# Row-maximum scores from 64 contracted rows, two query chunks side by side in the array, one maximum instruction for both

## The chip, the cores and the metric

The kernel runs on one core of one Trainium2 chip. The metric is the device time of one execution in microseconds (us), the median of several runs. A core has five engines with queues of their own: TensorE (PE, with its weight loads as PEld), VectorE (DVE), ScalarE (ACT), GpSimd (POOL) and SyncE (SP). They meet only at semaphores. Matrix products go to PSUM, which has eight banks of 512 fp32 values per partition; everything else lies in SBUF.

## The reference, cut to what matters

Two transformer blocks follow each other on 2 sequences of 512 tokens of width 128. The change touches the attention of the second one: 16 heads of 64 values, with a normalisation of every query and key.

```
qkv = (h @ Wqkv.T).reshape(b, n, 3, H, HD)
q = _ln(qkv[:, :, 0].transpose(0, 2, 1, 3), qn_g, qn_b)
k = _ln(qkv[:, :, 1].transpose(0, 2, 1, 3), kn_g, kn_b)
v = qkv[:, :, 2].transpose(0, 2, 1, 3)
scores = jnp.einsum('bhnd,bhmd->bhnm', q, k) / jnp.sqrt(jnp.float32(HD))
attn = jax.nn.softmax(scores, axis=-1)
o = jnp.einsum('bhnm,bhmd->bhnd', attn, v)
x = x + o.transpose(0, 2, 1, 3).reshape(b, n, H * HD) @ Wout.T
```

Before it stands a block with one attention head and a wide layer, behind it a gated choice of tokens for 8 experts. Neither is touched.

## The kernel before

The middle of the program, from about 85 to 350 us, handles 32 **units**: one head of one sequence each (`UNITS = 32`, sequences change every second unit). All engines run the same loop of units, each with an order of its own that is written out by hand in a function `time(u, r, head)`. Units 4 to 27 run in a counted loop whose body holds 12 units; the others are written out. In the turn of unit `u` the engines work on up to four neighbours at once: unit `u` gets its row maxima, unit `u-1` its probabilities and products with the values, unit `u-2` is added to the output, and the pieces `u+2` and `u+3` of later queries and keys are made. A **piece** holds two heads' queries and keys for half of the tokens, so a pair of units needs a pair of pieces.

What happens to a piece: `project` (L1426) multiplies tokens and weights in six matmuls; ACT takes squares (L637) and a copy (L643); DVE sums the squares (L977); POOL makes the scale (L484, L488) and applies it (L507); PE turns the result (`turn_piece`, L1231 called from L1436) into bank 1; ACT applies gain and bias (`piece_affine`, L660), which frees the bank and is told by the semaphore `kq_affine`. Keys lie in partitions 0 to 63 and queries in 64 to 127. DVE rounds both to the fast matmul type (`piece_high`, L991, into `k_s`); POOL takes what rounding left off (`piece_low`, L498); ACT copies the rounded queries to partitions 0 to 63 of `q_s` (`q_high`, L666) and the rounded keys to partitions 64 to 127 of `k_s` (`k_high_beside`, L683). So `q_s` holds high and low parts of the queries above each other, and `k_s` the high part of the keys twice.

What happens to a unit: `scores` (L1445) makes, for each of four chunks of 128 queries, one matmul of 128 contracted rows by 512 keys into bank 0; DVE takes the negated row maximum (`row_max`, L1003). With one bank, chunk `c+1` waits for the maximum of chunk `c` (`max_done`). When all four maxima are there, PE transposes them (`shifts`, L1453) into bank 1, and DVE writes them into the rows of `q_shift` (`shift_row`, L1010). `scores_T` (L1459 and L1464) makes the scores again, transposed and in full precision and already lowered by the maximum, into banks 2 and 3 in turn; ACT takes the exponential (L689); `mix` (L1474) multiplies by the values and sums in banks 4 and 5, 8 matmul instructions per call; DVE divides and adds (`unit_out`, L1020 and L1025).

What orders it all is each engine's own queue: PE starts its work strictly in the order of `time` (L1486), ACT in that of L691, DVE in that of L1032, POOL in that of L511.

Of the kernel before, what the change touches and what calls it, by code (L numbers as in the profile page):

```python
# [37 lines left out]
def film_attention_then_expert_choice(  # L38
# [35 lines left out]
    with ctx:  # L74
# [118 lines left out]

        moe = Area(loop2_start)
# [65 lines left out]
        o_rec_done = sem("o_rec_done")  # L260
# [287 lines left out]
        def _(act):  # L548
# [119 lines left out]

            def q_high_beside(p, p_in):

                wait(act, q_hi_moved, p + 1)
                wait(act, st_done, pair_free(p, p_in))
                act.activation(piece_at(q_shift, p_in, 0, HD), piece_at(q_s, p_in, 0, HD).bitcast(F32), ACT.Copy)\
                   .then_inc(q_beside, 1)

            def k_high_beside(p, p_in):

                if isinstance(p, int) and p in (0, 1, 3):
                    act.wait_ge(q_low_done, min(p + 1, 3))
                else:  # L680
                    wait(act, lows_done, 2 * p + 1)
                wait(act, q_hi_moved, p + 1)
                act.activation(piece_at(k_s, p_in, HD, P), piece_at(k_s, p_in, 0, HD).bitcast(F32), ACT.Copy)\  # L683
                   .then_inc(split_done, 1)
# [6 lines left out]
            def time(u, r, head):  # L691
# [18 lines left out]
                if turning:  # L710
                    q_high(u + 2, r + 2)
                if back:
                    keys_exp(u - 1, 3)
# [13 lines left out]
            q_high(0, 0)  # L727
            piece_affine(1)
            k_high_beside(0, 0)
            q_high(1, 1)  # L730
            k_high_beside(1, 1)
# [14 lines left out]
            q_high(2, 2)  # L746
            piece_square(4)
            piece_affine(3)
            keys_exp(0, 2)
            q_high(3, 3)  # L750
            k_high_beside(2, 2)
# [72 lines left out]
        def _(dve):  # L824
# [174 lines left out]
            def row_max(u, c):  # L999
                wait(dve, s_done, 4 * u + c + 1)  # L1000
                if c == 0:
                    wait(dve, shift_done, u)
                dve.tensor_reduce(negmax[:, c:c + 1], bank[0][:, :], AX, ALU.max, negate=True).then_inc(max_done, 1)  # L1003
# [28 lines left out]
            def time(u, r, head):  # L1032
                live, turning, leaving = due(u, 0, UNITS - 1), due(u, 0, UNITS - 3), due(u, 2, UNITS + 1)
                if live:
                    row_max(u, 0)
                if leaving:
                    unit_out(u - 2, r - 2, 0)
                if live:
                    row_max(u, 1)
                if leaving:  # L1040
                    unit_out(u - 2, r - 2, 1)
                if live:
                    row_max(u, 2)
                if due(u, 0, UNITS - 4):
                    piece_ss(u + 3)
                if turning:
                    piece_high(u + 2, r + 2)
                if live:
                    row_max(u, 3)
                    shift_row(u, r)  # L1050
# [16 lines left out]
            row_max(0, 1)  # L1067
            dve.wait_ge(h_act, 6)
            split_h(N + N // 2, TOK)
            row_max(0, 2)  # L1070
            piece_ss(2)
            row_max(0, 3)
            piece_ss(3)
            shift_row(0, 0)
            piece_norm(2, 2)
            row_max(1, 0)
            piece_norm(3, 3)
            piece_high(2, 2)
            row_max(1, 1)
            row_max(1, 2)  # L1080
# [3 lines left out]
            row_max(1, 3)  # L1084
# [142 lines left out]
        def _(pe):  # L1227
# [203 lines left out]
            def turn_piece(p, p_in):  # L1431

                wait(pe, normed, p + 1)
                wait(pe, kq_affine, p)
                wait(pe, shift_copied, p - 2)
                turn4(turn_bank(p), [qk_n[:, p_in % 2, 2 * c + h, :, :].rearrange("p t d -> p (t d)")  # L1436
                                     for h in range(2) for c in range(2)]).then_inc(kqT_done, 1)

            def scores(u, r, c):

                if c == 0:
                    wait(pe, split_done, u + 2 - r % 2)
# [43 lines left out]
            def time(u, r, head):  # L1486
                live, back = due(u, 0, UNITS - 1), due(u, 1, UNITS)
                if live:
                    scores(u, r, 0)
# [3 lines left out]
                if live:  # L1493
                    scores(u, r, 1)
# [5 lines left out]
                if live:  # L1500
                    scores(u, r, 2)
# [7 lines left out]
                if back:  # L1509
                    mix(u - 1, r - 1, 0)  # L1510
                    mix(u - 1, r - 1, 1)
                if live:
                    scores(u, r, 3)
                if back:
                    scores_T(u - 1, r - 1, 3)
                    mix(u - 1, r - 1, 2)
# [16 lines left out]
            keep_busy(1, bank[3])  # L1533
            scores(0, 0, 1)
            keep_busy(2, bank[3])
            pe.wait_ge(h_split, 3)
            project(2, 2, 0)
            scores(0, 0, 2)
            pe.wait_ge(h_split, 4)
            project(3, 3, 0)  # L1540
            scores(0, 0, 3)
            keep_busy(2, bank[3])
            shifts(0, 0)
            scores(1, 1, 0)
# [5 lines left out]
            scores(1, 1, 1)  # L1550
            project(4, 4, 2)
            turn_piece(3, 3)
            scores(1, 1, 2)
            scores_T(0, 0, 2)
            mix(0, 0, 0)
            mix(0, 0, 1)
            scores(1, 1, 3)
            scores_T(0, 0, 3)
# [209 lines left out]
```

## Time and profile before

| | |
|---|---|
| median of 3 runs | 431.98 us (431.81 to 432.7) |
| the profiled execution | 431.72 us |
| its span, first to last instruction | 430.0 us |
| granted TensorE clock, mean | 0.996 |
| PE busy | 405.9 us (94%), 2730 instructions |
| ACT busy | 284.7 us (66%) |
| DVE busy | 273.2 us (64%) |
| POOL busy | 191.9 us (45%) |

The shares are of the span. PE's busy time counts a matmul from its start to a modelled end, and matmuls overlap, so it hides small gaps; the distance between the starts of neighbours tells more. A row of the timeline merges instructions of one kind that follow without a gap: its start, the time to the end of the last, and the count.

### The profile page before, as it was taken

To read this page: it belongs to the slowest core of one execution; us is meant where nothing else is said; L and a number is where in the kernel's file an instruction comes from. 1 tells how busy PE (TensorE), PEld (TensorE's weight loads), DVE (VectorE), ACT (ScalarE), POOL (GpSimd) and SP (SyncE) were. 2 spreads that over 40 slices of the span, in tenths; PEclk is the share of its full clock that TensorE was granted. 3 is DMA by queue.
4 is the path that set the end of the run, shared out by engine and by line. 5 is a ranking of instruction groups with operands and counts; after the bars stand their busy time and mean duration, and the time that the engine had idled before them with its cause. 6 is when DMAs were issued, how large, how long until landed. Compare 5 with 4: busy or idle time off the path is not lost.

```text
span 430.0 us, 8319 instructions
## 1 busy us (share of the span) xinstructions
PE 405.9 (94%) x2730; PEld 341.3 (79%) x2730; DVE 273.2 (64%) x649; ACT 284.7 (66%) x532; POOL 191.9 (45%) x197
## 2 busy tenths in 40 slices
PE   6989997999999999999999999999999897889896
PEld 5678666778888888889888888888888686666694
DVE  3566456767666766666666667666765627986633
ACT  3356566677777777777777777777776337759341
POOL 7400416485566756765765667567656000100000
PEclk9899999999999999999999999999999999999999
DMA  6760000190000000000000000000000000000001
GB/s 128 205 135 1 2 2 0 54 366 23 0 3 2 0 2 1 3 0 2 3 2 0 0 0 1 0 0 0 1 0 2 0 2 1 2 2 2 1 2 49
DMA packets 7792, 10.67 MB, mean 25 GB/s; under 512 B 403, under 2 KB 4302, under 8 KB 7758
## 3 DMA queue, kind: packets, MB, share of 16 engines
q1 hardware_dynamic: 6718, 9.73, 7.9%
q10 hardware_dynamic: 1040, 0.52, 0.4%
q8 instruction: 17, 0.28, 0.3%
q14 instruction: 17, 0.14, 0.1%
HBM read 8.68 MB, written 0.52 MB: 21 GB/s over the span
## 4 chain that ended last, share of the span: by engine, by line
PE 82%; DVE 9%; POOL 4%; issue 2%; ACT 2%; DVEq 0%; POOLq 0%; ACTq 0%
PE pair L1474 26%; PE pair L1426 10%; PE pair L1445 8%; PE bank L1464 6%; PE bank L1459 6%; PE pair L1231 4%; PE pair L1706 2%; PE pair L1315 1%; PE pair L1600 1%; PE pair L1391 1%; PE bank L1231 1%; POOL rstd L453 1%; PE pair L1655 1%; PE pair L1340 1%; PE bank L1695 1%
## 5 line engine op out<-in xcount | busy, mean ns | idle before, releaser
L1474 PE MATMUL pair<-v_s,probs_T 128*128 128x129 f32 x1024 | 128.4, 275 | 0.6 <-ACT probs_T L689 0.6
L1474 PEld LDWEIGHTS pair<-v_s,probs_T 128*128 128x128 f32 x1024 | 124.5, 191 | 4.7 <-ACT probs_T L689 0.9
L1003 DVE TENSOR_REDUCE negmax<-pair 128x1 f32<-128x512 f32 x128 | 88.2, 689 | 50.1 <-PE pair L1445 49.9
L689 ACT ACTIVATE probs_T<-bank 128x512 f32<-128x512 f32 x128 | 73.1, 596 | 49.7 <-PE bank L1464 39.5
L498 POOL TENSOR_TENSOR q_s<-kq,k_s 64x512 fp32r<-64x512 f32 x29 | 37.2, 1283 | 78.0 <-DVE k_s L991 78.0
L1445 PE MATMUL pair<-k_s,q_s 128*128 128x512 f32 x128 | 59.4, 464 | 2.5 <-DVE negmax L1003 2.5
L488 POOL TENSOR_TENSOR qk_rstd<-qk_ms,minus_half 128x8 f32<-128x8 f32 x32 | 53.1, 1661 | 2.6 <-POOL qk_ms L484 0.2
L1459 PE MATMUL bank<-q_s,k_s 128*128 128x512 f32 x128 | 50.9, 397 | 0.0
L1464 PE MATMUL bank<-q_shift,k_low 128*128 128x512 f32 x128 | 50.6, 396 | 0.2 <-DVE q_shift L1010 0.2
L1025 DVE SCALAR_TENSOR_TENSOR x_att<-pair,o_rec,x_att 128x128 f32<-128x128 f32 x128 | 38.6, 345 | 1.1
L498 POOL TENSOR_TENSOR k_low<-kq,k_s 64x512 fp32r<-64x512 f32 x29 | 36.7, 1266 | 2.2
L1010 DVE TENSOR_TENSOR q_shift<-pair,own_chunk 4x512 fp32r<-4x512 f32 x32 | 21.8, 682 | 23.9 <-PE pair L1453 23.9
L1445 PEld LDWEIGHTS pair<-k_s,q_s 128*128 128x128 f32 x128 | 24.2, 189 | 13.5 <-DVE negmax L1003 12.3
L507 POOL TENSOR_TENSOR qk_n<-qk_raw,qk_rstd 128x512 f32<-128x512 f32 x28 | 29.3, 1045 | 2.4 <-POOL qk_rstd L488 0.5
L637 ACT ACTIVATE qk_sq<-pair 128x512 f32<-128x512 f32 x32 | 19.1, 598 | 16.4 <-PE pair L1426 16.3
L1464 PEld LDWEIGHTS bank<-q_shift,k_low 128*128 128x128 f32 x128 | 24.1, 188 | 5.8 <-issue 0.4
L1459 PEld LDWEIGHTS bank<-q_s,k_s 128*128 128x128 f32 x128 | 24.3, 190 | 2.6
L1426 PE MATMUL pair<-w_hi,h_hi 128*128 (+1 forms) x64 | 26.1, 408 | 0.0
L660 ACT ACTIVATE kq<-pair,cols 128x512 f32<-128x512 f32 x29 | 22.6, 778 | 4.9 <-PE pair L1231 1.7
L1426 PE MATMUL pair<-w_hi,h_lo 128*128 (+1 forms) x64 | 25.2, 393 | 0.0
L1426 PE MATMUL pair<-w_lo,h_hi 128*128 (+1 forms) x64 | 25.1, 392 | 0.0
L977 DVE TENSOR_REDUCE qk_ss<-qk_sq 128x8 f32<-128x512 f32 x32 | 21.7, 677 | 2.7 <-ACT qk_sq L637 2.7
(290 smaller groups left out, 699.3 us busy)
## 6 DMA issues: line engine op xcount, KB each, us to landing
fc_raw<-in_L_cond_fc2s_dram SPq DMA_DIRECT2D x1, 2048.0 KB, 14.0
x_in<-in_x_dram ACTq DMA_DIRECT2D x1, 512.0 KB, 3.9
w<-in_L_cond_mlp_w_dram SPq DMA_DIRECT2D x2, 256.0 KB, 2.9
wout<-in_L_cond_Wout_dram SPq DMA_DIRECT2D x1, 512.0 KB
k_low<-k_low SPq DMA_DIRECT2D x1, 512.0 KB, 8.2
q_shift<-q_shift SPq DMA_DIRECT2D x1, 512.0 KB, 10.7
b_all<-in_L_cond_b2s_dram SPq DMA_DIRECT2D x1, 512.0 KB, 10.7
out_dram<-final SPq DMA_DIRECT2D x2, 256.0 KB, 2.2
```

The costliest lines, as they stand in the source:

```text
L488: pool.tensor_tensor(qk_rstd[:, p_in % 2, :, :].rearrange("p c t -> p (c t)"), qk_ms[:, :, :].rearrange("p c t -> p (c t)"), minus_half[:, ...
L498: pool.tensor_tensor(piece_at(dst, p_in, lo, hi), kq32[lo:hi, :, :], piece_at(k_s, p_in, lo, hi).bitcast(F32), ALU.subtract)\
L507: pool.tensor_tensor(qk_n[:, p_in % 2, :, :, :], qk_raw[:, p_in % 2, :, :].rearrange("p c (t d) -> p c t d", d=HD), spread(qk_rstd[:, p_in ...
L660: act.activation(kq_from(p).rearrange("p h n -> p (h n)"), turn_bank(p)[:, :], ACT.Identity, bias=col("kq_b"), scale=col("kq_g")).then_inc ...
L689: act.activation(probs_T[:, k % 2, :], bank[2 + k % 2][:, :], ACT.Exp).then_inc(exp_done, 1)
L1003: dve.tensor_reduce(negmax[:, c:c + 1], bank[0][:, :], AX, ALU.max, negate=True).then_inc(max_done, 1)
L1025: last = dve.scalar_tensor_tensor(out=at, in0=pair4[:, half, t * (D + 1):t * (D + 1) + D], scalar=o_rec[:, c:c + 1], in1=at, op0=ALU.mult, ...
L1426: last = pe.matmul(banks_of(p)[:, c, :], h_part[:, at:at + P], w_part[:, bass.ds(head, 2), :].rearrange("p h w -> p (h w)"), start=(n == 0 ...
L1445: pe.matmul(bank[0][:, :], q_s[:, pair_at, h, c * P:c * P + P], k_s[:, pair_at, h, :], start=True, stop=True).then_inc(s_done, 1)
L1459: pe.matmul(bank[2 + k % 2][:, :], k_s[:, pair_at, h, at], q_s[:, pair_at, h, :], start=True, stop=False)
L1464: pe.matmul(bank[2 + k % 2][:, :], k_low[:, pair_at, h, at], q_shift[:, pair_at, h, :], start=False, stop=True).then_inc(st_done, 1)
L1474: last = pe.matmul(pair4[:, c // 2, c % 2 * (D + 1):(c % 2 + 1) * (D + 1)], probs_T[:, k % 2, c * P:c * P + P], v_s[:, r % (2 * PAIRS), k, :],
```

## The change

The scores that serve only the row maxima are made from the high parts alone, 64 contracted rows instead of 128. Two chunks of queries are issued next to each other: an even chunk from partitions 0 to 63 of `q_s` and `k_s` into bank 0, an odd chunk from partitions 64 to 127 of a new tile `q_up` and of `k_s` into bank 1. DVE takes both maxima in one instruction over the two banks. ACT fills `q_up` with a copy of the odd chunks' queries (`q_up_odd`), once per piece, and `k_high_beside`, which overwrites their source, waits for it. Since bank 1 is also the bank of `turn_piece` and of the transposed maxima, `scores` now waits for `shift_copied` in the first half and for `kq_affine` in the second, and `turn_piece` for the first maximum.

PE issues, per unit, two pairs where it issued four single matmuls, and the order of the other work around them is changed; on DVE the output of unit `u-2` now comes ahead of the first maximum.

```diff
+        q_up = Area(area_start)("q_up", [P, 2, 2, N // 2], F32R)
...
+            def q_up_odd(p, p_in):
+
+                wait(act, highs_done, p + 1)
+                wait(act, s_done, 2 * (p - 2 - p_in % 2))
+                first = p_in % 2 * (N // 2) + P
+                act.activation(q_up[HD:P, p_in // 2 % 2, :, p_in % 2 * P:p_in % 2 * P + P],
+                               k_s[HD:P, p_in // 2 % PAIRS, :, first:first + P].bitcast(F32), ACT.Copy)\
+                   .then_inc(q_raised, 1)
+
...
                 wait(act, q_hi_moved, p + 1)
+                wait(act, q_raised, p + 1)
                 act.activation(piece_at(k_s, p_in, HD, P), piece_at(k_s, p_in, 0, HD).bitcast(F32), ACT.Copy)\
                    .then_inc(split_done, 1)
...
                     q_high(u + 2, r + 2)
+                    q_up_odd(u + 2, r + 2)
...
-            def row_max(u, c):
-                wait(dve, s_done, 4 * u + c + 1)
-                if c == 0:
+            def row_max(u, half):
+                wait(dve, s_done, 2 * u + half + 1)
+                if half == 0:
                     wait(dve, shift_done, u)
-                dve.tensor_reduce(negmax[:, c:c + 1], bank[0][:, :], AX, ALU.max, negate=True).then_inc(max_done, 1)
+                dve.tensor_reduce(negmax[:, 2 * half:2 * half + 2], pair0[:, :, :], AX, ALU.max, negate=True)\
+                   .then_inc(max_done, 1)
...
+                if leaving:
+                    unit_out(u - 2, r - 2, 0)
+                    unit_out(u - 2, r - 2, 1)
                 if live:
                     row_max(u, 0)
-                if leaving:
-                    unit_out(u - 2, r - 2, 0)
-                if live:
-                    row_max(u, 1)
-                if leaving:
-                    unit_out(u - 2, r - 2, 1)
-                if live:
-                    row_max(u, 2)
                 if due(u, 0, UNITS - 4):
                     piece_ss(u + 3)
                 if turning:
                     piece_high(u + 2, r + 2)
                 if live:
-                    row_max(u, 3)
+                    row_max(u, 1)
                     shift_row(u, r)
...
                 wait(pe, shift_copied, p - 2)
+                wait(pe, max_done, 2 * (p - 2) + 1)
                 turn4(turn_bank(p), [qk_n[:, p_in % 2, 2 * c + h, :, :].rearrange("p t d -> p (t d)")
...
-            def scores(u, r, c):
-
-                if c == 0:
+            def scores(u, r, half):
+
+                if half == 0:
                     wait(pe, split_done, u + 2 - r % 2)
-                wait(pe, max_done, 4 * u + c)
-                pair_at, h = r // 2 % PAIRS, r % 2
-                pe.matmul(bank[0][:, :], q_s[:, pair_at, h, c * P:c * P + P], k_s[:, pair_at, h, :],
+                    wait(pe, shift_copied, u)
+                    if isinstance(u, int) and u == 1:
+                        pe.wait_ge(kq_affine, 3)
+                elif not (isinstance(u, int) and u == 0):
+                    wait(pe, kq_affine, (u + 3) if due(u, 0, UNITS - 3) else UNITS)
+                wait(pe, max_done, 2 * u + half)
+                pair_at, h, at = r // 2 % PAIRS, r % 2, 2 * half * P
+                pe.matmul(bank[0][:, :], q_s[0:HD, pair_at, h, at:at + P], k_s[0:HD, pair_at, h, :],
+                          start=True, stop=True)
+                pe.matmul(bank[1][:, :], q_up[HD:P, r // 2 % 2, h, half * P:half * P + P], k_s[HD:P, pair_at, h, :],
                           start=True, stop=True).then_inc(s_done, 1)
...
-                wait(pe, max_done, 4 * u + 4)
-                if not (isinstance(u, int) and u == 0):
-                    wait(pe, kq_affine, (u + 3) if due(u, 0, UNITS - 3) else UNITS)
+                wait(pe, max_done, 2 * u + 2)
                 pe.transpose(bank[1][0:NC, 0:P], negmax[:, :], ident[:, :]).then_inc(shift_done, 1)
```

The order of the calls in PE's `time` moves as well (the first pair stands behind the first two `scores_T`, the second between `mix` 0 and `scores_T` 3, and `mix` 1 moves behind `scores_T` 3), and the units 0 and 1 in front of the loop are reordered in the same sense. The rows below show the first full unit, `u = 2`.

PE at the start of a unit in the kernel before; `pair<-k_s,q_s` are the scores for the maxima, `bank<-` rows are `scores_T`, `w_hi,h_hi` rows are `project`:

```order
L1445 MATMUL pair<-k_s,q_s 128x512
L1459 MATMUL bank<-q_s,k_s 128x512
L1464 MATMUL bank<-q_shift,k_low 128x512
L1459 MATMUL bank<-q_s,k_s 128x512
L1464 MATMUL bank<-q_shift,k_low 128x512
L1445 MATMUL pair<-k_s,q_s 128x512
L1426 MATMUL pair<-w_hi,h_hi 128x512
```

The same place in the changed kernel, where `q_up` is the odd chunk:

```order
L1474 MATMUL bank<-q_s,k_s 128x512
L1479 MATMUL bank<-q_shift,k_low 128x512
L1474 MATMUL bank<-q_s,k_s 128x512
L1479 MATMUL bank<-q_shift,k_low 128x512
L1460 MATMUL pair<-k_s,q_s 128x512
L1462 MATMUL pair<-k_s,q_up 128x512
L1435 MATMUL pair<-w_hi,h_hi 128x512
```

The first chunk's scores moved behind the four matmuls of `scores_T`, next to the second chunk's.

PE in the second half of the unit, in the kernel before, from the last matmul of `project`; `ident,qk_n` is `turn_piece`, `v_s,probs_T` is `mix`, `ident,negmax` the transposed maxima:

```order
L1426 MATMUL pair<-w_hi,h_lo 128x512
L1445 MATMUL pair<-k_s,q_s 128x512
L1459 MATMUL bank<-q_s,k_s 128x512
L1464 MATMUL bank<-q_shift,k_low 128x512
L1231 MATMUL pair<-ident,qk_n 128x128 x4
L1474 MATMUL pair<-v_s,probs_T 128x129 x8
L1445 MATMUL pair<-k_s,q_s 128x512
L1459 MATMUL bank<-q_s,k_s 128x512
L1464 MATMUL bank<-q_shift,k_low 128x512
L1474 MATMUL pair<-v_s,probs_T 128x129 x4
L1453 MATMUL pair<-ident,negmax 4x128
L1474 MATMUL pair<-v_s,probs_T 128x129 x4
```

The same stretch in the changed kernel:

```order
L1435 MATMUL pair<-w_hi,h_lo 128x512
L1474 MATMUL bank<-q_s,k_s 128x512
L1479 MATMUL bank<-q_shift,k_low 128x512
L1240 MATMUL pair<-ident,qk_n 128x128 x4
L1489 MATMUL pair<-v_s,probs_T 128x129 x4
L1460 MATMUL pair<-k_s,q_s 128x512
L1462 MATMUL pair<-k_s,q_up 128x512
L1474 MATMUL bank<-q_s,k_s 128x512
L1479 MATMUL bank<-q_shift,k_low 128x512
L1489 MATMUL pair<-v_s,probs_T 128x129 x8
L1468 MATMUL pair<-ident,negmax 4x128
L1489 MATMUL pair<-v_s,probs_T 128x129 x4
```

Between `turn_piece` and the next scores stands one `mix` call where there were two, and the call that left stands behind `scores_T`. A row of `mix` counts each matmul of the source once; the trace has two instructions for each.

## Rows read from the trace of the kernel before

**Rows 1.** The page: chain that ended last by engine, and two groups of DVE.

```profile
PE 82%; DVE 9%; POOL 4%; issue 2%; ACT 2%; DVEq 0%; POOLq 0%; ACTq 0%
...
L1003 DVE TENSOR_REDUCE negmax<-pair 128x1 f32<-128x512 f32 x128 | 88.2, 689 | 50.1 <-PE pair L1445 49.9
...
L1025 DVE SCALAR_TENSOR_TENSOR x_att<-pair,o_rec,x_att 128x128 f32<-128x128 f32 x128 | 38.6, 345 | 1.1
```

**Rows 2.** PE's timeline over one unit: start us, us, instructions.

```profile
204.60 1.05 PE L1474 MATMUL pair<-v_s,probs_T 128*128 128x129 f32 x8
205.49 0.27 PE L1453 MATMUL pair<-ident,negmax 128*4 128x128 f32 x1
205.60 1.06 PE L1474 MATMUL pair<-v_s,probs_T 128*128 128x129 f32 x8
206.41 0.48 PE L1445 MATMUL pair<-k_s,q_s 128*128 128x512 f32 x1
206.73 0.39 PE L1459 MATMUL bank<-q_s,k_s 128*128 128x512 f32 x1
206.96 0.39 PE L1464 MATMUL bank<-q_shift,k_low 128*128 128x512 f32 x1
...
207.68 0.51 PE L1445 MATMUL pair<-k_s,q_s 128*128 128x512 f32 x1
208.02 0.48 PE L1426 MATMUL pair<-w_hi,h_hi 128*128 x1
...
209.26 0.40 PE L1426 MATMUL pair<-w_hi,h_lo 128*128 x1
...
210.19 0.60 PE L1231 MATMUL pair<-ident,qk_n 128*128 128x128 f32 x4
```

**Rows 3.** Timeline: transposed maxima of units 2 and 28; weight loads' waits between them.

```profile
104.04 0.27 PE L1453 MATMUL pair<-ident,negmax 128*4 128x128 f32 x1
...
323.76 0.27 PE L1453 MATMUL pair<-ident,negmax 128*4 128x128 f32 x1
...
PEld pair L1445 <- DVE negmax L1003: 7.5, 26, 0.3
```

**Rows 4.** PE's timeline around matmuls of 64 rows (L1356), entering and leaving.

```profile
55.46 0.28 PE L1391 MATMUL pair<-w,u 128*128 128x128 f32 x1
55.67 0.37 PE L1356 MATMUL pair<-wout_T,wqkv_raw 64*128 64x128 f32 x1
...
57.11 0.27 PE L1356 MATMUL pair<-wout_T,wqkv_raw 64*128 64x128 f32 x1
57.31 0.70 PE L1383 MATMUL bank<-h_T,w 128*128 128x512 f32 x1
```

**Rows 5.** The same line merged: rows 64 to 127 alone; then both halves.

```profile
50.42 1.16 PE L1356 MATMUL pair<-wout_T,wqkv_raw 64*128 64x128 f32 x8
...
55.67 1.71 PE L1356 MATMUL pair<-wout_T,wqkv_raw 64*128 64x128 f32 x16
```

**Rows 6.** ACT's timeline in the unit of rows 2.

```profile
209.69 0.60 ACT L637 ACTIVATE qk_sq<-pair 128x512 f32<-128x512 f32 x1 [0.63 <-PE pair L1426]
210.19 0.59 ACT L643 ACTIVATE qk_raw<-pair 128x512 f32<-128x512 f32 x1
210.91 0.78 ACT L660 ACTIVATE kq<-pair,cols 128x512 f32<-128x512 f32 x1
...
212.40 0.63 ACT L666 ACTIVATE q_s<-k_s 64x512 fp32r<-64x512 f32 x1
```

**Rows 7.** DVE's timeline in that unit, and a maximum over 64 elements.

```profile
205.80 0.68 DVE L1010 TENSOR_TENSOR q_shift<-pair,own_chunk 4x512 fp32r<-4x512 f32 x1 [0.77 <-PE pair L1453]
...
206.93 0.69 DVE L1003 TENSOR_REDUCE negmax<-pair 128x1 f32<-128x512 f32 x1 [0.45 <-PE pair L1445]
...
359.09 0.23 DVE L1101 TENSOR_REDUCE gate_m<-pair 128x8 f32<-128x64 f32 x1 [0.82 <-PE pair L1482]
```

**Rows 8.** PE's timeline in unit 31, third chunk of the scores.

```profile
343.07 0.50 PE L1445 MATMUL pair<-k_s,q_s 128*128 128x512 f32 x1 [0.83 <-DVE negmax L1003]
```

More of the change, by code:

```diff
@@ L259, in film_attention_then_expert_choice @@
                              "o_normed"))
-        o_rec_done = sem("o_rec_done")
+        o_rec_done, q_raised = sem("o_rec_done"), sem("q_raised")
         sq_summed, last_out = sem("sq_summed"), sem("last_out")
@@ L727, in _ @@
             q_high(0, 0)
+            q_up_odd(0, 0)
             piece_affine(1)
@@ L730, in _ @@
             q_high(1, 1)
+            q_up_odd(1, 1)
             k_high_beside(1, 1)
@@ L746, in _ @@
             q_high(2, 2)
+            q_up_odd(2, 2)
             piece_square(4)
@@ L750, in _ @@
             q_high(3, 3)
+            q_up_odd(3, 3)
             k_high_beside(2, 2)
@@ L1066, in _ @@
             split_h(N, N + N // 2)
-            row_max(0, 1)
             dve.wait_ge(h_act, 6)
             split_h(N + N // 2, TOK)
-            row_max(0, 2)
+            row_max(0, 1)
             piece_ss(2)
-            row_max(0, 3)
+            shift_row(0, 0)
             piece_ss(3)
-            shift_row(0, 0)
             piece_norm(2, 2)
-            row_max(1, 0)
             piece_norm(3, 3)
             piece_high(2, 2)
-            row_max(1, 1)
-            row_max(1, 2)
+            row_max(1, 0)
             piece_ss(4)
@@ L1083, in _ @@
             low_here(3, HD, q_s).then_inc(q_low_done, 1)
-            row_max(1, 3)
+            row_max(1, 1)
             shift_row(1, 1)
@@ L1487, in time @@
                 live, back = due(u, 0, UNITS - 1), due(u, 1, UNITS)
-                if live:
-                    scores(u, r, 0)
                 if back:
@@ L1493, in time @@
                 if live:
-                    scores(u, r, 1)
+                    scores(u, r, 0)
                 if isinstance(u, int) and u == UNITS:
@@ L1499, in time @@
                     project(u + 3, r + 3, head)
-                if live:
-                    scores(u, r, 2)
                 if back:
@@ L1510, in time @@
                     mix(u - 1, r - 1, 0)
-                    mix(u - 1, r - 1, 1)
                 if live:
-                    scores(u, r, 3)
+                    scores(u, r, 1)
                 if back:
                     scores_T(u - 1, r - 1, 3)
+                    mix(u - 1, r - 1, 1)
                     mix(u - 1, r - 1, 2)
@@ L1532, in _ @@
             pe.wait_ge(kq_affine, 2)
-            keep_busy(1, bank[3])
+            keep_busy(3, bank[3])
             scores(0, 0, 1)
-            keep_busy(2, bank[3])
             pe.wait_ge(h_split, 3)
             project(2, 2, 0)
-            scores(0, 0, 2)
+            shifts(0, 0)
             pe.wait_ge(h_split, 4)
             project(3, 3, 0)
[L1541 to L1544, printed above, removed]
             keep_busy(1, bank[3])
@@ L1549, in _ @@
             scores_T(0, 0, 1)
-            scores(1, 1, 1)
+            scores(1, 1, 0)
             project(4, 4, 2)
             turn_piece(3, 3)
-            scores(1, 1, 2)
             scores_T(0, 0, 2)
             mix(0, 0, 0)
+            scores(1, 1, 1)
+            scores_T(0, 0, 3)
             mix(0, 0, 1)
-            scores(1, 1, 3)
-            scores_T(0, 0, 3)
             mix(0, 0, 2)
```

## The prediction

> **What bounds the kernel now.** I read the chain of waits first: PE holds 82% of what ended last [rows 1]. Then PE's timeline over one unit [rows 2], where the reader should look at the distance between starts, not at durations. A `mix` instruction takes 0.11 us (eight from 204.60 to 205.49), one of 512 columns 0.23 (206.73 to 206.96), one of `turn_piece` 0.11. A unit has 32 `mix` instructions (3.57), 8 of `scores_T`, 6 of `project` and 4 of `scores` (18 x 0.2315 = 4.17), the turn (0.43) and the transposed maxima (0.11): 8.28 us. Units 2 to 28 follow each other in (323.76 - 104.04)/26 = 8.45 us [rows 3], most in about 8.41. So PE is full to within 0.13 to 0.17 us. The missing part shows at 207.68: the second chunk waits for the first maximum, and the next start comes 0.34 later instead of 0.23 [rows 2]; the table of waits has 26 such stops in 26 units [rows 3]. The 50 us that DVE waits for scores [rows 1] cost nothing. ACT and DVE have room, so what counts is what the change does to PE's row of starts, and which wait the new order puts into it.
>
> **What goes.** Four scores matmuls become two pairs. If a pair costs what one matmul costs, 2 x 0.23 = 0.46 us per unit go. Whether halves of the array run at once can be read from the few 64-row matmuls in this program [rows 5]: eight on rows 64 to 127 take 1.16 us; sixteen, first on rows 0 to 63 and then on 64 to 127, take 1.71, where one behind the other would take 1.16 + 8 x 0.11 = 2.05. So some three of eight ran beside the other half's. I take the pair at the price of one. The stop at the second chunk (0.13) goes too: the maximum of the first pair is wanted only by `turn_piece`, 1.85 us of matmuls later.
>
> **What comes: the switch of the array.** The same line shows what a step from 128 rows to 64 costs [rows 4]. Between neighbours of one kind the distance is 0.11; from the last 128-row matmul (55.46) to the first of 64 rows it is 0.21, and that one lasts 0.37 instead of its usual 0.27, since its weights were not loaded ahead. That is 0.10 + 0.10 = 0.20 us. On the way out it is the same: 57.11 to 57.31 is 0.09 over the distance, and the weight load is bare again (the first scores after a stop last 0.51 against 0.39 for a neighbour that had none [rows 2], so about 0.11). Behind a 512-column matmul the weight load would start some 0.08 over the usual distance, so I take 0.19 per step. Each pair is entered from 128-row work and left to it, in both places of the unit: 4 steps of 0.19 = 0.76 us against the 0.46 that go. Bounds: nothing, if the step can be hidden, and 0.20 each; I take the rows' value, because no work stands in the queue that could cover a step. A net of +0.30 per unit, and with the stop of 0.13 gone, +0.17.
>
> A rule speaks to this. [Rows 2] show that the transposed maxima, which use 4 output columns, are entered and left at the plain 0.11, while [rows 4] show a stop when the contracted rows change. The Trainium skill, page TensorEngine Tiling (Array Packing), section Key Properties, says that changing the tiling mode, not just the tile, drains the engine. By that rule alone the transposed maxima would pay as well if they change the mode; the trace agrees for the rows and not for the columns. The sum stands on the rows either way.
>
> **What comes: a wait for bank 1.** The second pair writes bank 1, so it waits for `kq_affine` of the piece turned just before. I follow both engines from the start p of `project`'s last matmul. ACT: squares at p + 0.43, copy at p + 0.93, both as now (209.26 to 209.69 and 210.19 [rows 6]); the copy ends at p + 1.52, and the turn, 0.23 earlier than now because the third chunk has left, is no longer what ACT waits for; gain and bias take 0.78, to p + 2.31; with 0.05 of semaphore (the maximum of 206.93 ends at 207.62, PE goes on at 207.68 [rows 2, 7]) p + 2.36. PE: two `scores_T` matmuls and the turn, then one `mix` call, whose last instruction starts at p + 1.91; the switched weight load could start at p + 2.11. So PE stops for 0.25 us in every unit. Behind the stopped instruction stand `scores_T` 3, `mix` 1 and 2 and the maxima, nothing of which another engine is short of. Bounds: 0, if ACT starts earlier than I think, to 0.4, if the copy is late.
>
> **Other edits.** DVE's maximum over 1024 values: 0.69 us for 512 [rows 1] and 0.23 for 64 [rows 7] give 1.03 ns per value, so 1.22 instead of 2 x 0.69. With the output first (a reciprocal and four additions of 0.345 [rows 1], together up to 1.6 us, from 0.2 us into the unit) the first maximum ends 2.85 to 3.05 us into the unit, and the turn wants it at 3.3: no stop in full units. `q_up_odd` is half of a 0.63 us copy [rows 6], about 0.41 on ACT, between `q_high` and the last exponential. The move of `mix` 1 makes that exponential wait for it: its start is 0.39 behind that of the last instruction of `mix` 1 (0.28 long, as the one in [rows 4], and ACT starts 0.12 behind a matmul's modelled end, 210.79 to 210.91 [rows 2, 6]), its length 0.60, the semaphore 0.05: 1.04 against the 1.0 us of `mix` 2 and the maxima on PE, a stop of about 0.04; ACT is through with `q_up_odd` 0.6 before. `shift_row` (0.31 behind the maxima, 0.68 long [rows 2, 7]) reaches `scores_T` of the next unit within 0.04 too, since the scores that stood ahead have left. I count 0.04 once; if the cover is thinner, up to 0.15. POOL loses nothing: its round of a piece, from turn to next turn, gets longer by as much as the unit.
>
> **The sum.** Per full unit +0.17 + 0.25 + 0.04 = 0.46, so 8.41 to 8.87. Units 2 to 28 are 27: +12.4. Unit 29 has a turn and no `project`, and stops for the maximum: +0.2. Units 30 and 31 have neither; there PE stands idle 0.83 [rows 8] for the second maximum, a stop that the new order covers with `scores_T` and `mix`: -0.8 each. Units 0 and 1, where much waits for other things: +0.4, between -1 and +1. In all +12.4 + 0.2 - 1.6 + 0.4 = +11.4. The profiled execution took 431.72 (span 430.0 and 1.7 around it), 0.26 under the median: 431.72 + 11.4 + 0.26 = 443.4 us.
>
> **Rivals.**
> *The steps cost nothing* (0 of 4 x 0.19; this is the side of faster). The unit then has 8.28 - 0.46 = 7.82 of matmuls. But ACT's dates don't move: the second pair could start 0.2 sooner after one `mix` call and waits 0.34 for `kq_affine`, and the last exponential adds 0.1 to 0.15. That is 8.31, only 0.1 under now; 27 x -0.1, and -1.3 in each of the last two units: -5, so 427 us. It decides the sign once four steps cost under some 0.25 us together. Against it: rows 4, in and out; for it, the free steps of the transposed maxima in rows 2. Chance 0.10.
> *The wait for bank 1 is hidden.* If ACT takes up gain and bias 0.25 earlier, only +0.2 per unit stays: 27 x 0.21 - 1 = +4.7, so 437 us. For it: ACT stands idle 0.63 before the squares [rows 6]; against it: the squares wait for `project`, which nothing moves. Chance 0.16.
> *The halves don't run beside each other*, because two 512-column matmuls were never paired here: 64 x 0.23 = 14.7 more, 458 us. Against it: rows 5. Chance 0.05.
> *No change.* Steps at a third of the rows' price would balance what goes; chance 0.03.
>
> **How the numbers follow.** Forecast: 443.4 us, chance 0.60, and 439 to 449 by the bounds of the stops and steps (0.10 us per unit is 2.7 us). The hidden wait reaches down to 435. Faster 0.10, no change 0.03, above 449 some 0.11 (halves in turn, or several small stops at once). 435 to 449 leaves out about 0.2. Within 0.2% (0.9 us) is what a measurement of this kernel can't tell from no change. Faster by more than that: 0.10; within: 0.03; slower: 0.87.
>
> **What would show it.** Right: transposed maxima 8.8 to 8.9 us apart in the full units; in PE's timeline the first `project` matmul some 0.42 behind the pair and the weight load of a pair 0.3 behind the last `scores_T`; the two starts of a pair together; a wait of the second pair for `kq_affine` in nearly every unit, and none for the maxima. Wrong: pairs at 0.23 from their neighbours (no step), 0.46 within a pair (no concurrence), or a unit in which the wait names the exponential or the maximum.

## The result, and the profile after

The changed kernel takes 438.94 us (median of 4 runs, 438.67 to 439.29) against 432.34 us (4 runs, 431.81 to 432.75) for the kernel before: a ratio of 1.0167 with an interval of 1.0138 to 1.0196. It is slower by 6.6 us, where the forecast said 11.4. The profiled execution took 438.67 us, its span is 436.9 where it was 430.0, and the granted clock was 0.994 of the upper level (2.4 GHz).

The page shows the change of character first: the chain that ended last, by engine; then two groups (busy us, mean ns of one, idle before).

```profile
PE 71%; ACT 12%; DVE 9%; POOL 4%; issue 3%; DVEq 0%; ACTq 0%; POOLq 0%
...
L1020 DVE TENSOR_REDUCE negmax<-pair 128x2 f32<-128x1024 f32 x64 | 78.3, 1224 | 5.8 <-PE pair L1462 1.5
...
L1460 PE MATMUL pair<-k_s,q_s 64*128 64x512 f32 x64 | 32.0, 500 | 2.4 <-ACT kq L662 0.6
```

PE held 82% of the chain [rows 1] and now holds 71%; ACT went from 2% to 12%. The maximum over 1024 values takes 1224 ns, where 1.22 us was forecast, and DVE's 50.1 us of waiting for scores [rows 1] have become 5.8. None of this says where 6.6 us went, since DVE is not short of time. PE's timeline over one unit does (start us, us), as in [rows 2]:

```profile
209.79 0.27 PE L1468 MATMUL pair<-ident,negmax 128*4 128x128 f32 x1
...
211.51 0.40 PE L1479 MATMUL bank<-q_shift,k_low 128*128 128x512 f32 x1
211.83 0.49 PE L1460 MATMUL pair<-k_s,q_s 64*128 64x512 f32 x1
211.84 0.49 PE L1462 MATMUL pair<-k_s,q_up 64*128 64x512 f32 x1
212.26 0.50 PE L1435 MATMUL pair<-w_hi,h_hi 128*128 x1
212.59 0.39 PE L1435 MATMUL pair<-w_lo,h_hi 128*128 x1
...
213.52 0.39 PE L1435 MATMUL pair<-w_hi,h_lo 128*128 x1
...
214.23 0.60 PE L1240 MATMUL pair<-ident,qk_n 128*128 128x128 f32 x4
214.66 1.06 PE L1489 MATMUL pair<-v_s,probs_T 128*128 128x129 f32 x8
215.78 0.50 PE L1460 MATMUL pair<-k_s,q_s 64*128 64x512 f32 x1
215.78 0.50 PE L1462 MATMUL pair<-k_s,q_up 64*128 64x512 f32 x1
216.21 0.50 PE L1474 MATMUL bank<-q_s,k_s 128*128 128x512 f32 x1
...
218.56 0.27 PE L1468 MATMUL pair<-ident,negmax 128*4 128x128 f32 x1
```

Read the starts. The two matmuls of a pair begin at 211.83 and 211.84: the halves do work at once. But the pair begins 0.32 behind the last `scores_T`, the first `project` 0.43 behind the pair, and the second `project` another 0.33 behind that, where two 512-column neighbours that neither wait nor step are 0.23 apart in [rows 2] (206.73 to 206.96). The three make 1.08 (211.51 to 212.59); three plain distances are 0.69. So two steps of the array cost 0.39 at this place, and one matmul of 0.23 fewer pays for a little over half of it: +0.16.

The transposed maxima of units 2 and 28, and the weight loads' waits between them, answer to [rows 3] (line waited for: us in total, times, longest):

```profile
104.78 0.27 PE L1468 MATMUL pair<-ident,negmax 128*4 128x128 f32 x1
...
332.35 0.27 PE L1468 MATMUL pair<-ident,negmax 128*4 128x128 f32 x1
```

```profile
PEld pair L1460 <- issue: 9.4, 26, 0.4
PEld pair L1460 <- ACT kq L662: 6.6, 26, 0.3
PEld pair L1435 <- issue: 6.3, 26, 0.2
PEld bank L1474 <- issue: 6.3, 26, 0.2
```

A unit takes (332.35 - 104.78)/26 = 8.753 us, against 8.451 before: +0.302, and 26 distances make +7.9. Up to unit 2 the kernel loses 0.7 (104.78 against 104.04), at unit 29 it loses 0.1, and units 30 and 31 take 6.80 each where they took 7.68 and 7.69, so 1.8 come back. Together +6.9, which is the difference of the spans. Three of the four rows of waits are "issue": nothing that the profile shows was waited for, and these are the steps, in and out, 26 times each. The remaining row is the second pair's wait for `kq_affine`, in which its step in lies too. The 26 stops for the first maximum [rows 3] are gone.

The 0.7 up to unit 2 has parts of both signs, and the clock is in both. The page's row of the granted clock (tenths, 40 slices of some 11 us), before and changed:

```profile
PEclk9899999999999999999999999999999999999999
PEclk9999999989999999999999999999999999999999
```

In the profiled execution of the kernel before, the clock stood at the lower level (granted 0.5, 1.2 GHz) from 9.9 to 13.3 us, far ahead of all that the change touches; in that of the changed kernel it did not, and its first `turn_piece` starts at 68.45 where it started at 69.81. Nothing of the change has run by then, so these 1.4 us are not its doing. Behind them the changed kernel loses 2.1 up to unit 2. PE stands idle 1.45 us ahead of 85.27 and 0.60 ahead of a pair at 86.99, and from 87.1 to 90.4 its granted clock is 0.5: that pair and the six `project` matmuls behind it take 3.43 us up to the next start, where the pair at 98.06 and its six take 1.92 at the upper level. That is 1.5 of the 2.1. Eight of the nine profiled runs with the new order in front of the loop show such a stretch between 87 and 96 us, the two with the old order show none there; why the ninth has none is open.

### The profile page after: what moved, and what is told of

It is laid out like the page before. It is cut to its first block, busy times and chain, and to the rows that moved or that the text cites. A ratio compares the mean times of both kernels' runs of the same rounds, so it can differ in the third digit from the quotient of the medians.

```text
span 436.9 us, 8331 instructions
## 1 busy us (share of the span) xinstructions
PE 411.6 (94%) x2722; PEld 330.1 (76%) x2722; DVE 270.9 (62%) x585; ACT 295.1 (68%) x564; POOL 190.8 (44%) x197
## 4 chain that ended last, share of the span: by engine, by line
PE 71%; ACT 12%; DVE 9%; POOL 4%; issue 3%; DVEq 0%; ACTq 0%; POOLq 0%
PE pair L1489 21%; PE pair L1435 11%; PE bank L1474 7%; PE pair L1460 7%; PE bank L1479 5%; ACT kq L662 5%; ACT qk_sq L639 4%; ACT qk_raw L645 2%; PE pair L1711 1%; PE pair L1324 1%; PE pair L1240 1%; PE pair L1605 1%; PE pair L1400 1%; POOL qk_rstd L490 1%; PE bank L1240 1%
## 5 line engine op out<-in xcount | busy, mean ns | idle before, releaser
L1020 DVE TENSOR_REDUCE negmax<-pair 128x2 f32<-128x1024 f32 x64 | 78.3, 1224 | 5.8 <-PE pair L1462 1.5
L1474 PE MATMUL bank<-q_s,k_s 128*128 128x512 f32 x128 | 57.1, 446 | 0.0
L1043 DVE SCALAR_TENSOR_TENSOR x_att<-pair,o_rec,x_att 128x128 f32<-128x128 f32 x128 | 36.0, 344 | 1.1
L1460 PE MATMUL pair<-k_s,q_s 64*128 64x512 f32 x64 | 32.0, 500 | 2.4 <-ACT kq L662 0.6
L1462 PE MATMUL pair<-k_s,q_up 64*128 64x512 f32 x64 | 32.0, 500 | 0.0
L1435 PE MATMUL pair<-w_hi,h_hi 128*128 (+1 forms) x64 | 28.9, 451 | 0.0
L1460 PEld LDWEIGHTS pair<-k_s,q_s 64*128 64x128 f32 x64 | 11.7, 183 | 19.8 <-issue 12.1
```

Of the source, the lines that this page charges most:

```text
L1020: dve.tensor_reduce(negmax[:, 2 * half:2 * half + 2], pair0[:, :, :], AX, ALU.max, negate=True)\
L1043: last = dve.scalar_tensor_tensor(out=at, in0=pair4[:, half, t * (D + 1):t * (D + 1) + D], scalar=o_rec[:, c:c + 1], in1=at, op0=ALU.mult, ...
L1435: last = pe.matmul(banks_of(p)[:, c, :], h_part[:, at:at + P], w_part[:, bass.ds(head, 2), :].rearrange("p h w -> p (h w)"), start=(n == 0 ...
L1460: pe.matmul(bank[0][:, :], q_s[0:HD, pair_at, h, at:at + P], k_s[0:HD, pair_at, h, :], start=True, stop=True)
L1462: pe.matmul(bank[1][:, :], q_up[HD:P, r // 2 % 2, h, half * P:half * P + P], k_s[HD:P, pair_at, h, :], start=True, stop=True).then_inc(s_d ...
L1474: pe.matmul(bank[2 + k % 2][:, :], k_s[:, pair_at, h, at], q_s[:, pair_at, h, :], start=True, stop=False)
```

## The experiments

In all of them a unit is the distance of the transposed maxima in the full units (units 2 to 28, the mean of 26 distances), as above: 8.45 before and 8.75 changed. Medians are set against the kernel before on the same chip, which took 432.0 to 432.6 there.

**All 128 rows in the pairs** (changed kernel; only the half contraction undone, and the copy for it left out).

```diff
-                pe.matmul(bank[0][:, :], q_s[0:HD, pair_at, h, at:at + P], k_s[0:HD, pair_at, h, :],
+                pe.matmul(bank[0][:, :], q_s[:, pair_at, h, at:at + P], k_s[:, pair_at, h, :],
...
-                pe.matmul(bank[1][:, :], q_up[HD:P, r // 2 % 2, h, half * P:half * P + P], k_s[HD:P, pair_at, h, :],
+                pe.matmul(bank[1][:, :], q_s[:, pair_at, h, at + P:at + 2 * P], k_s[:, pair_at, h, :],
```

> The changed kernel with its order, its two banks and its one maximum instruction, but the pairs contract all 128 rows again (no step of the array, no concurrence, no copy for the odd chunks). Theory of the steps: the unit has its 8.28 us of matmuls back, the second pair stops for the bank some 0.22 us and shows its weight load, 0.1: 8.6 us per unit instead of 8.74, and 0.3 less in each of the last two units; 434 to 435 us. Rival, the coupling by bank 1 and the new order cost the time and the steps little: two matmuls more per pair's price, 2 x 0.23 per unit, so 450 us.

Measured: 435.66 us (434.06 to 436.83, 10 runs), ratio 1.0082 (1.0056 to 1.0109), unit 8.62. Without halves the changed kernel is faster than with them: two matmuls one behind the other cost PE less than one pair and its steps. PE's and ACT's timelines at the second pair:

```profile
213.87 1.06 PE L1473 MATMUL pair<-v_s,probs_T 128*128 128x129 f32 x8
214.98 0.50 PE L1444 MATMUL pair<-k_s,q_s 128*128 128x512 f32 x1
215.32 0.39 PE L1446 MATMUL pair<-k_s,q_s 128*128 128x512 f32 x1
```

```profile
213.17 0.60 ACT L638 ACTIVATE qk_sq<-pair 128x512 f32<-128x512 f32 x1 [0.63 <-PE pair L1419]
213.66 0.59 ACT L644 ACTIVATE qk_raw<-pair 128x512 f32<-128x512 f32 x1
214.15 0.78 ACT L661 ACTIVATE kq<-pair,cols 128x512 f32<-128x512 f32 x1
```

The bank is free when `kq` ends, at 214.93, and the second pair starts at 214.98. The last instruction of the `mix` call started at 213.87 + 7 x 0.11 = 214.64. The unit holds 8.28 us of matmuls, as before, and the rest, 0.34, is this one stop with its bare weight load: 214.64 + 0.11 would have been the next start, 214.98 was, and the pair's second matmul follows 0.34 behind its first instead of 0.23.

**Both matmuls of a pair on rows 0 to 63**, so that they can't run at once.

```diff
-                pe.matmul(bank[1][:, :], q_up[HD:P, r // 2 % 2, h, half * P:half * P + P], k_s[HD:P, pair_at, h, :],
+                pe.matmul(bank[1][:, :], q_s[0:HD, pair_at, h, at + P:at + 2 * P], k_s[0:HD, pair_at, h, :],
```

> The changed kernel, but both matmuls of a pair use rows 0 to 63 of the array (the odd chunk read from its place in q_s, the copy left out). Theory, the halves run beside each other: the second matmul of a pair now costs 0.22 us, 64 x 0.22 = 14 us over the changed kernel, 453 us, and transposed maxima 9.2 us apart. Rival, the pair never ran at once and the starts in the trace are only modelled: no difference, 439 us.

Measured: 456.0 us (453.09 to 456.52, 4 runs), ratio 1.0533 (1.0475 to 1.059), unit 9.22. PE's timeline:

```profile
212.18 0.40 PE L1463 MATMUL bank<-q_shift,k_low 128*128 128x512 f32 x1
212.50 0.49 PE L1444 MATMUL pair<-k_s,q_s 64*128 64x512 f32 x1
212.84 0.39 PE L1446 MATMUL pair<-k_s,q_s 64*128 64x512 f32 x1
213.16 0.50 PE L1419 MATMUL pair<-w_hi,h_hi 128*128 x1
213.50 0.40 PE L1419 MATMUL pair<-w_lo,h_hi 128*128 x1
```

The unit grows by 9.22 - 8.75 = 0.47, two plain distances of 0.23: what the halves at once save is one whole matmul per pair, no more and no less. The way in (0.32) is the same as in the changed kernel. The run is longer by more than that (456 against the 453 expected) in front of the loop: unit 2 comes 4.3 us later than in the changed kernel, 1.7 of it already at the first `turn_piece` (70.17 against 68.45), and from 85 to 110 us the granted clock is 0.86 against 0.93. The page TensorE: Matmul & The Clock Gate of the Trainium skill, section Part 3, says that matmuls on different rows of the array overlap and start about 4 ns apart; the changed kernel's trace agrees (211.83 and 211.84). Its rule for the span of such a pack, one matmul and 4 ns, says nothing of the way in and out, which the same rows put at 0.39.

**Single matmuls of 64 rows in the kernel before**, one edit: the four scores matmuls leave out the rows 64 to 127, in their old places.

```diff
-                pe.matmul(bank[0][:, :], q_s[:, pair_at, h, c * P:c * P + P], k_s[:, pair_at, h, :],
+                pe.matmul(bank[0][:, :], q_s[0:HD, pair_at, h, c * P:c * P + P], k_s[0:HD, pair_at, h, :],
```

> The kernel before, its order, its one bank and its four maxima, with one edit: the four scores matmuls contract rows 0 to 63 alone. Theory: each stands alone among 128-row matmuls, so a unit has eight steps of 0.17 to 0.19 us and saves nothing: 1.3 to 1.5 us more per unit, 9.8 to 9.95 us in the loop, 470 to 475 us. Rival, the loss of the changed kernel lies in the pair itself (two weight loads, two banks written at once): fewer rows alone cost nothing, 432 us.

Measured: 473.24 us (472.38 to 474.1, 2 runs), ratio 1.0938 (1.0899 to 1.0976), unit 9.85. Less work in the array, and 41 us more:

```profile
207.94 0.40 PE L1464 MATMUL bank<-q_shift,k_low 128*128 128x512 f32 x1
208.27 0.49 PE L1445 MATMUL pair<-k_s,q_s 64*128 64x512 f32 x1
208.69 0.50 PE L1426 MATMUL pair<-w_hi,h_hi 128*128 x1
209.03 0.39 PE L1426 MATMUL pair<-w_lo,h_hi 128*128 x1
```

The three distances, 0.33, 0.42 and 0.34, make 1.09 where plain ones make 0.69: 0.40 for two steps, as in the changed kernel. Four such visits are some 1.6 per unit; the unit grew by 1.40, and the old stop for a maximum (0.13 to 0.17) is covered by the longer unit: the maximum ends at 207.95, when the `scores_T` ahead starts, and the scores follow that start by 0.33, which is the way in and no more. This is the step's price alone, without pairs, copies, waits for bank 1 or a new order. The page TensorEngine Tiling (Array Packing) of the Trainium skill, section Key Properties, says that a change of the tiling mode drains the engine, without a price; here it is 0.20 us a step. That section would make the transposed maxima pay as well if four output columns are another mode; [rows 2] show them free.

**The second `mix` call ahead of the second pair** (changed kernel, in the loop).

```diff
                 if back:
                     mix(u - 1, r - 1, 0)
+                    mix(u - 1, r - 1, 1)
                 if live:
                     scores(u, r, 1)
                 if back:
                     scores_T(u - 1, r - 1, 3)
-                    mix(u - 1, r - 1, 1)
```

> The changed kernel with the second mix call put back ahead of the second pair, in the loop alone. Theory: the stop for bank 1 (0.13 us per unit) has cover, nothing else comes late, unit 8.62 us: 27 x 0.13 = 3.4 us less, 435.5 us. Rival, the maximum of the second pair then comes too late for the transposed maxima and the stop only moves: 439 us.

Measured: 435.1 us (434.15 to 438.21, 10 runs), ratio 1.0087 (1.006 to 1.0113), unit 8.62, and no weight load waits for `kq` any more. So the stop for bank 1 is worth 8.75 - 8.62 = 0.13 us per unit, and what is left over the 8.28 of matmuls, 0.34, are the steps net of the two matmuls saved.

**Two maxima instead of one** (changed kernel).

```diff
-                dve.tensor_reduce(negmax[:, 2 * half:2 * half + 2], pair0[:, :, :], AX, ALU.max, negate=True)\
-                   .then_inc(max_done, 1)
+                dve.tensor_reduce(negmax[:, 2 * half:2 * half + 1], bank[0][:, :], AX, ALU.max, negate=True)
+                dve.tensor_reduce(negmax[:, 2 * half + 1:2 * half + 2], bank[1][:, :], AX, ALU.max, negate=True)\
+                   .then_inc(max_done, 1)
```

> The changed kernel with two maximum instructions of 512 columns per pair instead of one of 1024. Theory: DVE has 0.31 us more per unit, but the first maximum still ends 0.3 us before the turn wants it and the second well before the transposed maxima; no difference, 439 us, within 0.3. Rival, the single instruction is part of what the change gained: up to 0.3 us per unit, 448 us.

Measured: 440.07 us (439.37 to 441.24, 4 runs), ratio 1.0195 (1.0146 to 1.0243), unit 8.75 to 8.76. Nothing in the loop; the span is 0.8 longer, more than the 0.3 expected, but 0.6 of it is there at the first `turn_piece` (69.05 against 68.45), ahead of every maximum, and so is not the edit's. So one instruction instead of two is worth nothing in the full units.

**All 128 rows and the second `mix` call ahead**, the two edits above together.

> Pairs of 128 contracted rows in two banks with one maximum instruction, and the second mix call ahead of the second pair in the loop: neither the step of the array nor the stop for bank 1. Theory: these two are all that the change loses, and what is left is a gain: the unit comes down to its matmuls, 8.28 to 8.32 us against 8.45 on average before (26 x 0.31 under the kernel with 128 rows and the stop, 435.7), and the last two units keep their 0.9 each; 427 us, 1.1% faster than before. Rival, something else in the new order holds the unit (the last exponential, or the maxima written back): 8.5 us or more per unit, 432 us or more.

Measured: 431.44 us (429.95 to 433.61, 12 runs), ratio 0.9987 (0.9963 to 1.0012), unit 8.46 (8.47 from the third distance on). A miss: without steps and without the stop for bank 1 the unit should have come to its 8.28. PE's timeline and DVE's show what stands in the way:

```profile
212.52 0.39 PE L1446 MATMUL pair<-k_s,q_s 128*128 128x512 f32 x1
...
213.22 1.05 PE L1473 MATMUL pair<-v_s,probs_T 128*128 128x129 f32 x8
214.24 0.27 PE L1452 MATMUL pair<-ident,negmax 128*4 128x128 f32 x1
214.34 1.13 PE L1473 MATMUL pair<-v_s,probs_T 128*128 128x129 f32 x8
```

```profile
212.96 1.23 DVE L1004 TENSOR_REDUCE negmax<-pair 128x2 f32<-128x1024 f32 x1 [0.93 <-PE pair L1446]
```

The maximum ends at 214.19 and the transposed maxima start at 214.24; behind the eight `mix` instructions they could have started at 213.22 + 8 x 0.11 = 214.1. The stop for bank 1 had been exchanged for one for the joint maximum, which ends 1.67 behind the pair's second start and now has only two `scores_T` matmuls and one `mix` call to hide it. With the stop (0.13) and a longer `mix` call behind it (1.13 against 1.05) the unit is back at 8.47.

**The same with the copy kept**: `q_up_odd` and the wait for it stay, though nothing reads the result. It answers whether the copy costs something that the first experiment had taken away with it.

> The kernel with 128-row pairs and the second mix call ahead, with ACT's copy of the odd chunks and the wait on it kept, though nothing reads the copy: the price of the copy by itself. Theory: ACT has room in every unit, so 0 in the loop; in front of the loop the copy stands on the way to the first scores, up to 0.8 us: 427 to 428 us. Rival, 0.41 us of ACT per unit count: 27 x 0.41 = 11 us more, 438 us.

Measured: 431.91 us (429.21 to 433.55, 10 runs), ratio 0.999 (0.9965 to 1.0015), unit 8.47. The copy is free. The time is above the 427 to 428 expected for the same reason as in the run before it.

**All 128 rows and the last `scores_T` ahead of the second pair**: the stop for bank 1 is covered from the front (0.46 us of `scores_T`), and two whole `mix` calls stand between the pair and the transposed maxima.

```diff
                 if back:
                     mix(u - 1, r - 1, 0)
+                    scores_T(u - 1, r - 1, 3)
                 if live:
                     scores(u, r, 1)
                 if back:
-                    scores_T(u - 1, r - 1, 3)
                     mix(u - 1, r - 1, 1)
```

> The changed kernel without its half contraction (all 128 rows in every score matmul, q_up not made), and with the last block of transposed scores ahead of the second pair, so that between mix call 0 and the second pair stand two matmuls of about 0.46 us together, and between the second pair and the transposed maxima two mix calls of about 2.0 us. Theory (the stop of 0.13 us for bank 1 and the second maximum's end 2.2 us after its pair are the two things that the full-row version with a mix call ahead traded against each other): both are covered now, the unit is 8.28 to 8.32 us, 0.16 under the 8.47 of that version, and the time is 426 to 428 us. Rival (the stop is not the affine's but a price of the pair after a mix call): the unit stays at 8.45 to 8.47 and the time at 431 to 432.

Measured: 426.63 us (424.52 to 426.8, 5 runs), ratio 0.9856 (0.9829 to 0.9883), unit 8.29. It beats the kernel before by 6.0 us and the changed one by about 12. Of the 5.1 us between the spans of the profiled executions (424.9 and 430.0) the full units give 4.3 and units 30 and 31 give 2.4; 1.6 are lost ahead of unit 2 and behind unit 31. The waits' table has no stop of PE left in the full units, and PE's timeline is one row of plain distances (behind a `mix` call these are 0.03 from its last instruction and then 0.32, in [rows 2] as well):

```profile
208.97 1.06 PE L1473 MATMUL pair<-v_s,probs_T 128*128 128x129 f32 x8
209.78 0.48 PE L1458 MATMUL bank<-q_s,k_s 128*128 128x512 f32 x1
210.09 0.40 PE L1463 MATMUL bank<-q_shift,k_low 128*128 128x512 f32 x1
210.33 0.40 PE L1444 MATMUL pair<-k_s,q_s 128*128 128x512 f32 x1
210.56 0.40 PE L1446 MATMUL pair<-k_s,q_s 128*128 128x512 f32 x1
210.79 1.95 PE L1473 MATMUL pair<-v_s,probs_T 128*128 128x129 f32 x16
212.58 0.27 PE L1452 MATMUL pair<-ident,negmax 128*4 128x128 f32 x1
```

**The same order with the changed kernel's halves**, to see whether a better order saves them.

> The changed kernel as it is (64 rows, two halves at once), with the last block of transposed scores ahead of the second pair in the loop. Theory: the stop for bank 1 goes as in the version with a mix call ahead (8.62 us a unit), the four array steps stay, and the second maximum is covered: unit 8.62, time about 435, that is still slower than before. Rival (the array steps are cheap and the order is what costs): unit 8.3, time about 427.

Measured: 435.5 us (434.88 to 436.77, 4 runs), ratio 1.0083 (1.0056 to 1.0111), unit 8.63. It does not: with every stop covered, the halves still cost 0.34 us per unit, and the two kernels of this order, which differ in nothing but the half contraction and its copy, lie 8.9 us apart. The waits' table still names `kq` at the second pair, but there `kq` ends at 214.37 and the pair starts at 214.76, 0.33 behind the `scores_T` ahead of it (214.44), as the first pair does: the way in and no stop.

## Why the prediction was right in direction and too large

**The pair and its steps: right.** +0.30 per unit was forecast, 4 x 0.19 for the steps against 0.46 for two matmuls. Measured: +0.34 (8.63 against 8.29 in the two kernels that differ in this and the free copy alone), and 0.39 to 0.40 for two steps where 0.38 was said. The price read from matmuls of 128 columns [rows 4] carries over to 512. The pair at the price of one was a guess that came out: [rows 5] gave "some three of eight" beside the other half, and in the pairs the two run wholly at once. The rival that the steps cost nothing falls with the "issue" rows; the one that the halves don't run at once falls with the second experiment, which is that rival built on purpose.

**The wait for bank 1: the term that was mis-sized.** It is there, in 26 of 26 units, by the name that was given, but it is 0.13 and not 0.25. PE's side was right: from `project`'s last start at 213.52 to the `mix` call's last instruction, 1.91 was forecast and 214.66 + 7 x 0.11 - 213.52 = 1.91 measured. ACT's side was wrong in one place (ACT's timeline in that unit):

```profile
213.95 0.60 ACT L639 ACTIVATE qk_sq<-pair 128x512 f32<-128x512 f32 x1 [0.81 <-PE pair L1435]
214.45 0.59 ACT L645 ACTIVATE qk_raw<-pair 128x512 f32<-128x512 f32 x1
214.94 0.78 ACT L662 ACTIVATE kq<-pair,cols 128x512 f32<-128x512 f32 x1
```

The squares start at p + 0.43 and the copy at p + 0.93, as said. Then the prediction put gain and bias behind the copy's end, at p + 1.53 (its 2.31 less 0.78); they start at p + 1.42, 0.49 behind the copy's start, though the copy lasts 0.59. ACT takes up an instruction some 0.1 us ahead of the end of the one before it, and this stood in [rows 6]: squares of 0.60 us at 209.69 and the copy at 210.19. The prediction used the 0.50 between these two and then the full 0.59 for the next. The page ScalarE: Activation LUTs of the Trainium skill, section What ACT_TABLE_LOAD costs, states an overlap of about 93 ns for neighbours; both traces agree with 0.10. So the pair starts at p + 2.26, not p + 2.36, and the stop is half as long. It also shows how the stop and the step share: the full-row version waits for the same date of `kq`, and its stop with the bare weight load costs 0.33, while with halves a step of 0.2 lies in the same time and only 0.13 is left over.

**The last exponential (0.04): not there.** In the full units no row of the waits names `probs_T` or `q_shift` for PE. `mix` 1 and 2, and then the last exponential on ACT:

```profile
216.78 1.95 PE L1489 MATMUL pair<-v_s,probs_T 128*128 128x129 f32 x16
```

```profile
217.93 0.60 ACT L701 ACTIVATE probs_T<-bank 128x512 f32<-128x512 f32 x1 [0.42 <-PE pair L1489]
```

The last instruction of `mix` 1 starts some seven distances of 0.11 in, at 217.56. The exponential follows 0.37 behind it and ends 0.97 behind it, where 0.99 was said. PE's side was miscounted: from that start to `mix` 3 there are the instruction's own 0.11, eight of `mix` 2 (0.89) and the maxima (0.11), 1.11 and not 1.0. That covers it.

**The base: 8.41 for most units, but 8.45 in the mean.** Both numbers stood in the text, and the sum took the smaller one. Some of the units before were longer by a little; the changed kernel's lie between 8.73 and 8.76 nearly throughout, so those extra hundredths went with the old stop. The gain from that stop is 8.45 - 8.28 = 0.17, not 0.13.

**Together**: +0.34 for pairs and steps, -0.17 for the old stop, +0.13 for the new one is +0.30, the 8.75 measured against 8.45. Against the forecast of 0.46 that is -0.12 for the new stop, -0.04 each for the exponential and the base, +0.04 for the steps: -0.16 a unit, 26 times 4.2 of the 4.5 us by which the forecast was too high. The tail was near: 0.1 at unit 29 (0.2 forecast), -1.8 in the last two (-1.6). The head came out near, +0.7 up to and with unit 2 against 0.4 + 0.46, by luck: it is -1.4 from a clock ahead of the change and +2.1 behind it, most of that a stretch at the lower clock, and the forecast had neither.

**The range.** 438.94 lies at the low edge of the forecast's own bounds, just under their 439, and inside them only as the rival of the hidden wait widens them, to 435. The unit, 8.75, lies under the 8.8 to 8.9 that was to show the forecast right; the other signs (0.42 behind the pair, 0.3 in front of it, two starts together, a wait for `kq_affine` in every unit) all came.

**The rival of a hidden wait** (437 us) was half right in size and wrong in its reason: ACT did take up gain and bias earlier, by 0.1 and through overlap, and the wait was halved rather than hidden. The time came out between that rival and the forecast.

**Not forecast at all**: that the order, not the array, held a gain. The stop for a maximum in the old order (0.17), the stop for bank 1 in the new one (0.13, and 0.33 with full rows) and the late joint maximum with a `mix` call moved (0.19) take each other's place, and the order with the last `scores_T` ahead avoids all three.

## What to carry to other kernels

Halving the contracted rows to run two matmuls side by side saves one matmul per pair and costs a step in and a step out; here 0.23 against 0.39. One pair of 512 columns, set between full-row work, is too little: at these prices a visit would pay from its second pair on (0.46 saved), by little, an estimate from the distances above that no run here tried. Before an array is reshaped, look at which stops the order leaves: the same joint maximum with full rows and one block of work moved gave 1.4% over the kernel before. When two engines' dates are followed to a hundredth, take the distance of starts on both, not the durations on one.

## What was not expected of the hardware

- A step between 128 and 64 contracted rows costs 0.19 to 0.20 us at both widths read (128 columns in [rows 4], 512 here), in parts of 0.10 at the first start and 0.10 at the distance behind it: the weight load is not taken ahead over a step but starts with its matmul, as the weight loads' timeline of the changed kernel shows for both halves. A step that only changes the output columns (the transposed maxima, 4 columns) costs nothing: 0.11 in and out, before and after.
- A stop and a step at the same place do not add up: waiting for the same `kq` costs 0.33 us a unit with full rows (0.22 of lateness and a bare weight load) and 0.13 on top of the step.
- ACT's 0.60 us instructions follow each other at 0.49 to 0.50.

The weight loads' timeline for the first of these points, beside PE's rows at the same times above:

```profile
211.83 0.18 PEld L1460 LDWEIGHTS pair<-k_s,q_s 64*128 64x128 f32 x1 [0.37 <-issue]
211.84 0.18 PEld L1462 LDWEIGHTS pair<-k_s,q_up 64*128 64x128 f32 x1
212.26 0.19 PEld L1435 LDWEIGHTS pair<-w_hi,h_hi 128*128 128x128 f32 x1 [0.24 <-issue]
212.37 0.19 PEld L1435 LDWEIGHTS pair<-w_lo,h_hi 128*128 128x128 f32 x1
```

The two loads of the pair and the first of `project` start with their matmuls (211.83, 211.84, 212.26); the second of `project` starts at 212.37, ahead of its matmul at 212.59, as loads do between neighbours of one kind.
